# One list for the second combination of expert rows, the sign-weight product and sparse attention, with the lowest expert's rows gathered inside the expert loop

## What is computed

```python
x = x + 0.5 * L0_ffn(LN(x))     # again, after retention
x = x + 0.5 * L1_ffn(LN(x))
x = x + L1_attn(LN(x))

# L0_ffn: 32 experts, six per token, C = CAP_FACTOR * (T * 6 // 32) rows each
topk_w, topk_idx = top_k(softmax(x @ wg_router.T), 6)
pos_in_e = ...                   # running count of the token in its expert
valid = pos_in_e < C
ye = (silu(xe @ w_gate) * (xe @ w_up)) @ w_down     # per expert
y = sum_i topk_w[i] * ye[idx_i, pos_i] * valid  +  shared expert
# L1_ffn
alpha = mean(abs(w), axis=1)
y = x @ (where(w >= 0, 1, -1) * alpha).T + bias
# L1_attn
importance = x @ Wi + bi         # one number per token
mask = importance > sorted_desc[102], or among the 32 largest of the sequence
k, v = (x @ Wk + bk) * mask, (x @ Wv + bv) * mask
y = softmax(q k^T / 4, 16 heads) v @ Wo + bo
```

## Time and profile before

| | |
|---|---|
| median of 3 runs | 1925.78 us (1925.01 to 1929.13) |
| span of the profiled execution | 1930.3 us |
| mean granted TensorE clock | 0.924 |
| busy share of the span | PE 87%, DVE 77%, ACT 62%, POOL 45% |
| stage 2 leaves its last expert | about 592 us |
| stage 3 | 608.5 to 671.5 us |
| stage 4, front | 671.5 to 704.7 us |
| stage 4, tile list | 704.7 to 786 us |
| stage 5 | 786 to 818.5 us |

### The profile page before, as it was taken

How to read it: one execution, slowest core, us unless ns; L and a number is a source line. 1 busy time by engine, 2 the same in 40 slices (tenths; PEclk the granted TensorE clock), 3 DMA queues, 4 the chain that set the end, 5 groups by cost and what they waited for, 6 DMA issues and landing times. The chain is left out here.

```text
span 1930.3 us, 29481 instructions
## 1 busy us (share of the span) xinstructions
PE 1682.2 (87%) x10866; PEld 1371.6 (71%) x10866; DVE 1476.8 (77%) x3059; ACT 1188.9 (62%) x2391; POOL 868.8 (45%) x854
## 2 busy tenths in 40 slices
PE   6899579978995567798879998889999999998899
PEld 4799247857993345696669787667777777776688
DVE  7888677667886677687778666788888888889666
ACT  4588246645881169416841543888888888888443
POOL 0775432105765500301531210267878878778411
PEclk9899779989997589798979998999999999999799
DMA  8797212315983200000010010000000100100111
GB/s 307 225 290 245 71 53 90 117 38 180 288 264 99 84 1 2 1 1 0 1 59 39 27 41 1 21 8 28 23 23 23 33 15 21 33 1 14 53 41 36
DMA packets 74605, 139.86 MB, mean 72 GB/s; under 512 B 11476, under 2 KB 52564, under 8 KB 73428
## 3 DMA queue, kind: packets, MB, share of 16 engines
q1 hardware_dynamic: 63700, 108.50, 17.2%
q0 software_dynamic: 10752, 29.37, 5.2%
HBM read 113.73 MB, written 24.12 MB: 71 GB/s over the span
## 5 line engine op out<-in xcount | busy, mean ns | idle before, releaser
L79 PE MATMUL ps<-H_r,wt_r 128*128 128x512 f32 (+1 forms) x732 | 287.1, 430 | 14.2 <-POOL wt_r L91 7.5
L91 DVE TENSOR_TENSOR work<-work,ps 128x512 f32<-128x512 f32 (+4 forms) x306 | 172.1, 562 | 108.3 <-ACT work L87 59.0
L79 PE MATMUL ps<-work_r 128*128 128x256 f32 (+2 forms) x1200 | 243.8, 294 | 6.5 <-DVE work_r L91 2.4
L87 ACT ACTIVATE work<-ps 128x512 f32<-128x512 f32 (+3 forms) x355 | 168.2, 496 | 127.3 <-PE ps L79 107.9
L79 PE MATMUL ps<-wt,work 128*128 128x256 f32 (+2 forms) x1144 | 224.8, 368 | 8.7 <-ACT work L87 5.9
L79 PEld LDWEIGHTS ps<-work_r 128*128 128x128 f32 (+1 forms) x1200 | 190.4, 188 | 20.8 <-DVE work_r L91 11.3
L79 PEld LDWEIGHTS ps<-wt,work 128*128 128x128 f32 (+1 forms) x1144 | 174.5, 199 | 37.9 <-ACT work L87 9.1
L79 PE MATMUL ps<-ering_r,work_r 128*128 128x256 f32 (+1 forms) x814 | 199.9, 314 | 0.4 <-ACT work L87 0.4
L99 DVE SCALAR_TENSOR_TENSOR wt<-ps,wt 128x511 f32<-128x511 f32 (+2 forms) x234 | 174.2, 747 | 22.9 <-ACT wt L87 17.2
L79 PEld LDWEIGHTS ps<-H_r,wt_r 128*128 128x128 f32 (+1 forms) x732 | 140.3, 192 | 71.3 <-issue 12.9
L87 ACT ACT_TABLE_LOAD x113 | 145.0, 1283 | 46.8 <-DVE lmv L119 28.3
(11 more groups left out here) (248 smaller groups left out, 4204.8 us busy)
## 6 DMA issues: line engine op xcount, KB each, us to landing
ering<-in_moe_w SPq DMA_DIRECT2D x87, 624.0 KB, 5.7
ye<-work SPq DMA_DIRECT2D x64, 256.0 KB, 5.1
wt<-in_ssd_wg SPq DMA_DIRECT2D x64, 128.0 KB, 2.2
ye<-early SPq DMA_DIRECT2D x1, 4096.0 KB, 14.5
wt<-in_ssd_wg SPq DMA_DIRECT2D x8, 512.0 KB, 3.6
Hd<-H SPq DMA_DIRECT2D x16, 128.0 KB, 1.7
wt<-in_ret_fc SPq DMA_DIRECT2D x2, 1024.0 KB, 12.2
work<-Hd,work POOLq DMA_INDIRECT x128, 4.2
```

Source lines behind the costliest of these rows:

```text
L79: self.last = self.e.matmul(o, l, r, start=start, stop=stop, skip_group_check=True)
L87: self.last = self.e.activation(o, a, f, **kw)
L91: self.last = self.e.tensor_tensor(o, a, b, op)
```

## The change

1. **Columns from the highest expert down.** The codes of a token's six experts come out of the top eight with the highest expert first, so column 5 is a token's lowest expert. It is gathered for all eight tiles in new steps "early" beside experts 30 and 31, from the part of `ye` up to expert 26, into `H`, with a semaphore of its own per tile. The other five columns go through the ring as before, column i waiting for the stores up to expert 31-i alone.
2. **Routing.** Capacity is kept by a minimum in segment 8; the products with drop and keep are gone, and `puts` is computed only in the branch for an overflowing expert. Segments 9 and 10 move from the place ahead of the loop into it, behind the "in" steps of experts 0 and 1.
3. **One list.** `mid_order` takes the place of the lists of stages 3 and 4. From it come the adds of tiles 2 to 7 one per step, `binned(t)`, `front(h)` per sequence (importance, columns, q, signs and comparisons, rank, places, picked rows, keys, values) and the attention tiles; attention of a tile may begin once the keys and values of its own sequence are there. There is no wait of all engines between the two stages. "turn" is split into "turning" (PE) and "turned" (copy), "mul" into "mul" (PE) and "muls" (DVE).
4. **Bias on PE.** In stages 3 and 5 a product of a one-hot column with `bin_b` opens the bank, DVE does one instruction less per tile, and `M3.tmp` is gone.
5. **Buffers and queues.** The exponentials and signs move out of `ering`; places and keys of one sequence share a bank. POOL fetches tiles 2 and 3 before the wait of all engines and tiles 4 to 7 behind its clears; SP loads the triangular matrix earlier.

The core of the diff:

```diff
+        COLUMNS = (5, 4, 3, 2, 1, 0)
...
-            todo.append(("half", si, 1, 9))
             todo.append(("slots", si))
             todo.append(("up", 33, 0))
-            todo.append(("half", si, 1, 10))
-            if si == 0:
-                todo += [("half", si, 0, seg) for seg in (9, 10)]
...
+                todo.append(("in", e))
+                if e < 2:
+                    todo.extend(("half", si, h, 9 + e) for h in ((1,) if si else (0, 1)))
+                elif e == 30:
+                    todo.extend(("early", si, t) for t in range(2))
+                elif e == 31:
+                    todo.extend(("early", si, t) for t in range(2, NT))
...
+        def mid_order(si):
+            todo, begun, early, ready, heads = [], set(), Steps(), set(), []
+            def gathered():
+                for k in range(12, 6 * NT):
+                    todo.append(("add", si - 1, k // 6, COLUMNS[k % 6]))
+                    if k % 6 == 5:
+                        early.live.append(binned(k // 6))
+                    yield
+            def binned(t):
+                todo.append(("na", si, t))
+                yield
+                todo.append(("nb", si, t))
+                todo.append(("turning", si, t))
+                yield
+                todo.append(("turned", si, t))
+                todo.append(("mul", t))
+                yield
+                todo.append(("muls", t))
+                todo.append(("na", si + 1, t))
+                yield
+                todo.append(("nb", si + 1, t))
+                todo.append(("turning", si + 1, t))
+                yield
+                todo.append(("turned", si + 1, t))
+                ready.add(t)
+                if ready >= set(range(HALF * (t // HALF), HALF * (t // HALF) + HALF)):
+                    early.live.append(front(t // HALF))
+            def front(h):
+                todo.append(("imp", h))
+                yield
+                todo.append(("imps", h))
+                todo.append(("q", h))
+                yield
+                todo.append(("sign", h))
+                for j in range(4):
+                    todo.append(("equal", h, j))
+                    if j % 2:
+                        yield
+                todo.append(("qs", h))
+                todo.append(("rank", h))
+                yield
+                todo.append(("before", h))
+                todo.append(("pos", h))
+                yield
+                todo.append(("picks", h))
+                todo.append(("hs", h))
+                yield
+                todo.append(("hss", h))
+                todo.append(("keys", h))
+                yield
+                todo.append(("kT", h))
+                yield
+                todo.append(("values", h))
+                heads.append(h)
...
+            early.live = [gathered(), binned(0), binned(1)]
+            while not heads:
+                early.step()
+            live = []
             for t in range(NT + 8):
+                if t == HALF:
+                    early.drain()
                 for age in (2, 0, 1, 3, 4, 5, 6, 7, 8, 9, 10):
                     if age == 0 and t < NT:
                         live.append(tile(t))
                     if 0 <= t - age < NT:
                         next(live[t - age], None)
+                    if t < HALF and age < 5:
+                        early.step()
+                        early.step()
...
-                v.tt(r.code, pos, bc(ecap[:, 0:32].unsqueeze(1), [128, n, 32]), ALU.add).then_inc(V)
+                v.stt(r.code, pos, CAP - 0.75, bc(ecap[:, 0:32].unsqueeze(1), [128, n, 32]), ALU.min, ALU.add).then_inc(V)
...
-                v.tt(r.code, r.code, drop, ALU.subtract).then_inc(V)
-                v.tt(r.codes, r.code, r.keep, ALU.mult).then_inc(V)
-                v.tt(r.codes, r.codes, drop, ALU.add).then_inc(V)
-                v.tt(r.codes, r.codes, r.sel, ALU.mult).then_inc(V)
+                v.tt(r.codes, r.code, r.sel, ALU.mult).then_inc(V)
...
+        def g_first(g, si, t):
+            rows_stored(g, si, 26)
+            g.gather(H[:, t, :], None, ye[0:27 * CAP, :], get[:, t, 5:6]).then_inc(s_first[t], "in", si, t, by=16)
...
+            for i in COLUMNS[1:]:
+                k = 5 * t + 4 - i
+                rows_stored(g, si, 31 - i)
+                g.wait_ge(PE, "out", si, 28)
                 if k >= NGB:
+                    g.wait_ge(V, "gathered", si, (k - NGB) // 5, 4 - (k - NGB) % 5)
+                g.gather(gb[k % NGB], None, ye[0:(32 - i) * CAP, :], get[:, t, i:i + 1]).then_inc(s_gb[k % NGB], "in", si, t, i, by=16)
...
+            pe.mm(b[:, 0:256], bc(ident[:, 0:1], [128, 128]), wts["bin_b"], True, False)
             need_hT(pe, si, [t])
             pe.wait_ge(A, "bwT")
             for c in range(2):
+                pe.mm(b[:, 0:256], hT[:, c, cols(t)], M3.bwT[:, c, :], False, c == 1)
...
-                    v.tt(q, b.ap[:, 0:256], wts["bin_b"], ALU.add).then_inc(V).frees(b)
-                    v.wait_ge(V)
-                    v.stt(X[:, t, :], q, 0.5, X[:, t, :], ALU.mult, ALU.add).then_inc(V, "X", si, t)
+            v.stt(X[:, t, :], b.ap[:, 0:256], 0.5, X[:, t, :], ALU.mult, ALU.add).then_inc(V, "X", si, t).frees(b)
```

499 lines of the change are left out of this document (270 added, 229 removed).

## The result

| | |
|---|---|
| changed kernel, median of 11 runs | 1938.91 us (1929.57 to 1943.39) |
| kernel before, median of 11 runs beside it | 1929.13 us (1925.01 to 1931.03) |
| ratio | 1.0056, 95% interval 1.0042 to 1.0070 |
| profiled span | 1939.5 us (before 1930.3) |
| predicted | 1940, range 1917 to 1952 |

A forecast was written before the change was run, and what follows sets the result against it. It saw no engine full in stage 3, with idle time in different engines up to tile 2's maxima, then ACT setting attention's pace. Routing -0.7, list stretch +11.1 (columns' -2.1 included) and stage 5 +3.5 gave +13.9: 1940 us, range 1917 to 1952.

The forecast's parts named there:

- Columns and routing, -2.1 and -0.7: Second expert stage's end: early column removes a 2.15 us gather wait, -2.1; routing instructions dropped, -0.35 per stage, -0.7.
- the first expert stage gives nothing from its gathers: First expert stage: DVE goes on at 210.12 without a wait, so early gathers give 0; at most 2.1.
- The list up to tile 2, +11.2 from its own start: Common list from 606.4 us: DVE work 79 plus waits 42, tile 2's maxima at 727.5 instead of 718.45.
- the keys of sequence 0: Front of sequence 0 in the list: DVE's wait for keys priced at 1.55 us, within 4.9 for that front.
- its signs: Common list: clock near 0.5 up to the first front, DVE waiting on PE before sums into X of tiles 2 to 7.
- The prices at half clock: List's tiles, PE at 1.2 GHz: transposes 0.69 us, bias 1.04, product 2.08; a lifted clock would take 12.2 off.
- Keys and values of sequence 1 between the maxima of tiles 2 and 3, +2.0: Attention: they add 2.0 us to the first step of 9.33; from there both orders have ACT's pace.
- rival 3, the ring binding again: List's adds wait on ring gathers as before, 9.0 us on top of the 42: 1949 us; chance 0.12.
- Bias on PE in stage 5, +3.5: Stage 5: two more PE records per tile lengthen a chain that PE ends, +3.5 us; ends +1 and +6.
- That the list lifts the clock: Stage 3: more PE work per us holds 2.4 GHz, six tiles save 12.2 us: 1925 us; chance 0.09.
- That it fills DVE: Up to tile 2's maxima: DVE share 0.80, stretch 99 us instead of 121, 1916 to 1918 us; chance 0.25.
- That ACT's pace gives back what was lost: Attention: ACT's 9.33 us per tile regains the list's loss, leaving +3.5 and -0.7: 1929 us; chance 0.05.

The follow-up runs named there:

- run 3: Kernel before with early columns, routing and bias on PE, all of the change but the common list with its buffers and queues: ratio 0.9949.
- run 2: Kernel before with only the bias of the sign-weight product moved to PE in stages 3 and 5: ratio 0.9975.
- run 1: Kernel before with only the columns from the highest expert down, early gathers and the routing edits: ratio 0.9955.
- run 4: Changed kernel with overwritten filling products on PE in the common list, three ahead of each wait for H, two ahead of each sign-weight product: ratio 1.0043.
- run 5: Changed kernel with the list written in the old order: tiles nine wide, then both sequences' fronts, then attention: ratio 0.9945.
- run 6: Changed kernel with two adds per step of the list instead of one: ratio 0.9991.
- run 7: Changed kernel with everything ahead of attention's tiles (adds, products, norms, both fronts) written before the first scores: ratio 1.0019.
- run 8: Changed kernel with two adds per step and everything ahead of attention's tiles before the first scores: ratio 0.9967.
- run 12: Changed kernel with two overwritten filling products on PE ahead of each wait for H in the common list: ratio 1.0023.
- run 11: Kernel before with one overwritten filling product on PE ahead of each sign-weight product in stages 3 and 5, DVE still adding the bias: ratio 0.9984.
- run 9: Changed kernel in the old list order, but with the front of sequence 1 placed between the scores of the first tiles: ratio 0.9976.
- run 10: Changed kernel in old list order, sequence 1's front between the first scores, sequence 0's front beginning once tile 3 has passed: ratio 0.9994.

## Why the prediction was right

The forecast was 1940 us and slower by 13.9; measured were 1938.91 and 10.8. Its main term was right by its mechanism, and two smaller ones were not. That the sum came so close is in part luck. Against run 3 the list costs 20.6 us where 13.2 (11.2 + 2.0) were forecast, 7.4 too little; everything beside it earns 9.8 where the forecast had a loss of 0.7 (-2.1 - 0.7 + 3.5), 10.5 too much. The two misses leave 3.1.

- **Columns and routing, -2.1 and -0.7.** -3.35 at the start of stage 3 in the two profiles, and the wait of 2.15 us is gone. One product of the second expert stage stands at 418.97 us in the kernel before and at 417.80 in the changed one. From it to the start of stage 3 it is 190.5 and 190.8 us in the kernel before and run 2, and 187.6 to 188.3 in the changed kernel and runs 1 and 3 to 8, 2.7 less. What lies ahead of it can't be told: the product itself stands at 415.4 to 420.0 us in these eight. So the first stage's share of routing stays open, and so does the forecast that the first expert stage gives nothing from its gathers: the product of 210.12 stands at 209.12, but at 209.7 to 211.2 in runs 1 to 8.
- **The list up to tile 2, +11.2 from its own start.** Measured +13.9. The waits came to 48.3 us instead of 42 (the 0.94 ahead of the first reduction counted, as in the forecast), DVE's work to 75.6 instead of 79. By groups, forecast and measured: start and tiles 0 and 1, 7.2 and 6.1; single file and late roots, 14.3 and 15.8; front 0, 4.9 and 8.8; maxima of tiles 0 and 1, 4.25 and 6.35; second front and tile 2, 11.6 and 11.2. The step that failed most is the keys of sequence 0, priced at 1.55: they waited 5.80 us, since the picked rows and the keys with values are 16 products each, 3.75 and 3.76 us at the 1.2 GHz level (1.95 and 2.02 at the 2.4 GHz level), with nothing written between them. Of its signs, the granted clock was 0.64 up to the first front, not near 0.5, and PE was waited for before four of the six sums of tiles 2 to 7. Runs 6, 7 and 8 confirm two causes that it names, single file with 12.5 us and roots and scores among norms with 7, together 17. The prices at half clock are confirmed only as far as run 12 goes: lifting it gave 6.4 us, but not in the distance between two sums.
- **Keys and values of sequence 1 between the maxima of tiles 2 and 3, +2.0.** Measured 11.32 against 9.33, 2.0. After it the pace is the same in both, as said.
- **What the missing gathers would have given.** The prediction took the list's start from the early column, but did not see that five rows in the ring also speed the tiles of stage 3, up to 9.5 us less to the last add (run 1). The list hid that: with one chain under way its adds waited for nothing, and its tiles were slow for another reason. Its rival 3, the ring binding again, was wrong the same way, with 0.4 us of waits. So the list's cost against run 3 is larger than forecast, and columns and routing are worth 8.7 us (run 1) instead of 2.8.
- **Bias on PE in stage 5, +3.5.** Wrong in sign: -2.2 in the profiles and -4.5 in run 2. "DVE loses an instruction of 0.42 per tile from a chain that PE ends" is the sentence that failed. In the kernel before DVE takes up the products of tiles 1 to 5 without a wait, and waits for PE only at tile 0 and at the last two; the 0.71 us of the earlier trace rows are the last of all, in a stretch (802.7 to 812 us) with a granted clock of 0.50. DVE's timeline of the kernel before, bias of tiles 5 and 6:

```profile
804.81 0.39 DVE L91 TENSOR_TENSOR work<-ps,wt 128x256 f32<-128x256 f32 x1
...
807.56 0.42 DVE L91 TENSOR_TENSOR work<-ps,wt 128x256 f32<-128x256 f32 x1 [0.21 <-PE ps L79]
```

So once a few tiles are under way, DVE ends the chain: in the changed kernel the distance between two of the last sums into X is its own instructions and 0.36 us behind a root. DVE's timeline of the changed kernel, sums of the first and the last two tiles in stage 5:

```profile
806.58 0.43 DVE L99 SCALAR_TENSOR_TENSOR X<-ps,X 128x256 f32<-128x256 f32 x1 [3.77 <-PE ps L79]
...
820.49 0.42 DVE L99 SCALAR_TENSOR_TENSOR X<-ps,X 128x256 f32<-128x256 f32 x1
...
822.48 0.41 DVE L99 SCALAR_TENSOR_TENSOR X<-ps,X 128x256 f32<-128x256 f32 x1
```

The last two stand 1.99 us apart, the first and the last 15.9; in the kernel before first and last were 18.3 apart (bias at 792.11 to bias at 810.44), in run 11, with the clock lifted and DVE's instruction kept, 17.3. The first sum comes 8.35 us behind attention's last sum, before 6.99. How much of that is PE's records is open, for run 1, which has none of them, shows 7.94.
- **The rivals.** That the list lifts the clock was half true at the start (0.64 instead of 0.54, but 0.61 in run 3 without the list) and false at the end (0.55 instead of 0.75 or more). That it fills DVE was false: 0.58, where 0.765 was the point from which it decides. That ACT's pace gives back what was lost was false too: from tile 3 to the last sum 57.9 us, before 57.8. The single file's forecast of slower held by the order of the list alone (run 5).

Of the tables: the trace has 117 loads, four more as counted. The load at 702.64 begins 0.02 us behind the activation ahead of it, and the root at 703.94 0.02 us behind the end of the load. So the drain that the Trainium skill ("ScalarE: Activation LUTs", "What ACT_TABLE_LOAD costs") adds to a load does not stand in these rows either. What the loads cost came by their place: two of them stand with their root behind a tile's exponentials, 5.8 us, and DVE waited 2.92 us (682.32) and 4.08 us (704.26) for the roots.

## What to carry to other kernels

Merging two stages into one list didn't fill idle time by itself; the number of chains under way counted for more, so before a list is written step by step, count for each engine how many independent tiles stand between a step and the step that waits for it: here one add against a hand-over of some four us lost 12 us, and twice as many adds per step won them back. In runs 9 and 10 a serial front written between other work was moved, not hidden. An instruction saved on the engine that sets the pace of a pipelined stage can be worth about its length per tile, even if it adds work to an engine that looks as busy: here eight instructions of 0.42 us, 3.4 us, gave 1.6 us at the least. To see which engine that is, read the waits of several tiles in the middle of the stage, not those of its last one.

## What the runs showed of the hardware

- Filling products that change nothing lifted PE's granted clock in the list from 0.64 and 0.77 to 0.91 and 0.89 (run 4), with no gain clear of noise (0.13%). Fewer of them, all ahead of the wait for H (run 12), gave 0.85 and 0.94 and 6.4 us.
- Filling records and the clock that they lifted were worth 0.5 us in 33 together (run 11: 0.69 to 0.85), since DVE set the pace for most tiles.
- The same 16 products took 3.75 us and 1.95 us in one execution (656.15 and 722.43, changed kernel), with a granted clock of 0.50 and of 1.00.
- A square root behind a table load of 1.28 us began 0.02 us after the load's end (703.94, changed kernel).
- DVE's write of H in stage 5 of the changed kernel takes 0.41 us for most of the last tiles, but 0.93 to 1.38 us between 808 and 816 us, where POOL is busy 7.75 of 8.00 us and two sums stand 2.5 to 3.0 us apart instead of 1.99. Whether POOL's work is the reason no run tests.
- The rest of the program behind stage 5, the same code in all runs, took 1108.3 to 1111.5 us in the fourteen profiles. The -1.3 at the end of the first table lies within that.
- One chip of those used was 1.2% slower for the same kernel (1948.9 against 1926.6 us, medians). In runs 9, 10 and 12, on that chip, the excess lies ahead of stage 3, which starts at 626.7 to 627.6 us instead of 603.0 to 607.9.
